# A two-layer graph network with 49 source tiles in place of 50, and one condition an engine at the end

## The reference

```python
# layer 0
h = x @ W + b_W;  xi, xj = split(h, 2)
m = (xj[src] + ea @ W_e + b_We) / (in_degree[dst] + 1e-6)
x1 = layernorm(x + xi + segment_sum(m, dst))
# layer 1: graph convolution with self loops, batch norm over the nodes, leaky ReLU
h = x1 @ W1
dinv = rsqrt(in_degree + 1)
o = segment_sum(h[src] * dinv[src] * dinv[dst], dst) + b1      # self loops included
y = (o - mean) * rsqrt(var + 1e-5) * gamma + beta
out = layernorm(x1 + where(y >= 0, y, 0.01 * y))
```

## Time and profile before

| | |
|---|---|
| median of three runs | 948.84 us (948.3 to 949.46) |
| profiled execution | 947.83 us, span 946.0 us |
| PE busy (matmul) | 895.1 us, 95% of the span, 12296 instructions |
| PE weight loads | 800.0 us, 85% |
| DVE busy | 686.1 us, 73% |
| ACT busy | 465.0 us, 49% |
| POOL busy | 406.1 us, 43% |
| mean granted clock of PE | 0.989 of full speed |
| DMA | 247.94 MB, mean 262 GB/s |

### The profile page before, as it was taken

The page is one execution under the profiler, slowest core; times in us unless marked ns, Lnnn a source line. Parts: engine busy times, 40 slices in busy tenths (PEclk is TensorE's granted clock), DMA queues, the critical chain, the costliest instruction groups (busy, mean ns, idle before and its releaser), DMA issues.

```text
span 946.0 us, 31072 instructions
## 1 busy us (share of the span) xinstructions
PE 895.1 (95%) x12296; PEld 800.0 (85%) x12296; DVE 686.1 (73%) x1587; ACT 465.0 (49%) x991; POOL 406.1 (43%) x495
## 2 busy tenths in 40 slices
PE   5688999999999999999999999999999999999994
PEld 4577888888988988999999999999988988888863
DVE  5898999999999988899888889888822111112254
ACT  3775666666666665566565556566532000000045
POOL 3546755767766654355434445434330110111100
PEclk9899999999999999999999999999999999999997
DMA  5657989888888887777777677779463987788544
GB/s 163 215 210 233 378 296 375 303 311 312 301 287 314 289 310 243 257 246 237 249 265 279 220 256 236 223 266 312 160 262 120 401 321 272 263 294 322 203 146 135
DMA packets 95686, 247.94 MB, mean 262 GB/s; under 512 B 41128, under 2 KB 63356, under 8 KB 89644
## 3 DMA queue, kind: packets, MB, share of 16 engines
q1 hardware_dynamic: 92268, 240.58, 72.4%
q0 software_dynamic: 2400, 4.88, 1.5%
q10 hardware_dynamic: 864, 0.39, 0.2%
HBM read 185.46 MB, written 60.35 MB: 260 GB/s over the span
## 4 chain that ended last, share of the span: by engine, by line
PE 85%; DVE 7%; ACT 3%; DMA 2%; issue 2%; POOL 1%; ACTq 0%; DVEq 0%; POOLq 0%
PE x_ps L809 26%; PE pair_ps L873 19%; PE pair_ps L791 14%; PE e_ps L828 10%; PE x_ps L817 9%; PE j_ps L855 2%; DVE lo_oh L561 2%; DVE key_oh L564 2%; DMA rows<-in_dst,row_i 1%; PE pair_ps L882 1%; PE j_ps L856 1%; ACT counts L993 1%; PE u_vps L1357 1%; DMA xsplit<-in_dst 1%; ACT u_xo L1273 1%
## 5 line engine op out<-in xcount | busy, mean ns | idle before, releaser
L993 ACT CAST counts<-pair_ps 128x800 bf16<-128x800 f32 x391 | 319.5, 830 | 252.0 <-PE pair_ps L791 234.8
L809 PE MATMUL x_ps<-counts,xsplit 128*128 128x256 bf16 (+1 forms) x2500 | 310.9, 270 | 0.0
L561 DVE TENSOR_TENSOR lo_oh<-counter,lo_t 128x1024 bf16<-128x1024 bf16 x391 | 273.3, 699 | 49.9 <-PE pair_ps L791 47.9
L809 PEld LDWEIGHTS x_ps<-counts,xsplit 128*128 128x128 f16 x2500 | 225.7, 97 | 29.8 <-issue 7.9
L564 DVE TENSOR_TENSOR key_oh<-counter,key_t 128x800 bf16<-128x800 bf16 x391 | 233.0, 596 | 0.0
L791 PE MATMUL pair_ps<-key_oh,lo_oh 128*128 128x100 bf16 x3128 | 205.3, 208 | 13.4 <-DVE key_oh L564 6.1
L791 PEld LDWEIGHTS pair_ps<-key_oh,lo_oh 128*128 128x128 bf16 x3128 | 180.2, 97 | 28.6 <-DVE key_oh L564 10.7
L828 PE MATMUL e_ps<-streams 128*32 128x128 f32 x3528 | 108.5, 277 | 0.5 <-issue 0.5
L817 PE MATMUL x_ps<-counts,zown 128*128 128x256 bf16 (+1 forms) x840 | 103.2, 269 | 0.0
L873 PE MATMUL pair_ps<-streams,zown 128*128 128x256 bf16 x904 | 101.8, 273 | 0.0
L828 PEld LDWEIGHTS e_ps<-streams 128*32 128x32 f32 x3528 | 95.0, 111 | 5.4 <-issue 1.5
(11 more groups left out here) (174 smaller groups left out, 881.7 us busy)
## 6 DMA issues: line engine op xcount, KB each, us to landing
streams<-in_edge_attr SPq DMA_DIRECT2D x196, 576.0 KB
counts_kept<-counts SPq DMA_DIRECT2D x10, 1664.0 KB, 8.7
streams<-counts_kept SPq DMA_DIRECT2D x6, 1664.0 KB, 7.0
counts<-counts_kept SPq DMA_DIRECT2D x4, 1664.0 KB, 7.6
counts_kept<-counts SPq DMA_DIRECT2D x2, 3200.0 KB, 13.0
streams<-counts_kept SPq DMA_DIRECT2D x2, 3200.0 KB, 14.6
dinv_row<-dinv_rows SPq DMA_DIRECT2D x25, 128.0 KB, 5.3
edst<-in_dst SPq DMA_DIRECT2D x196, 4.5 KB
```

Source lines behind the costliest of these rows:

```text
L561: dv.tensor_tensor(lo_oh[:, at % RING, :, :, :], counter[:, :, :].unsqueeze(1).to_broadcast([P, SW // 2, P, 2]), pairs(lo_t[b % 2][:, w]). ...
L809: last = nc.tensor.matmul(x_ps[:, 0, 0:n], xsplit[:, q // 2, q % 2, :], by_hi[:, q // 2, :], start=(q == 0), stop=(q == 2 * HI - 1))
L993: a.copy(out.rearrange("p h (g n) -> p h g n", g=2), pair_ps[at % 2][:, :, 0:4 * KW].rearrange("p g (n h) -> p h g n", h=HI)).then_inc(S[" ...
```

## The change

The last block's even and odd nodes go into one tile: even nodes in its partitions 0 to 52, odd ones in 64 to 116. There are HS = 49 tiles, KW = 98 values of the key and 98 passes a block. A key of tile 49 (an odd node of the last block) is drawn to tile 48 with `min`, and 64 is added to its lo. So `make_keys` changes: `dl` is multiplied by HS at once, hi and parity are added first, `upper` marks the odd nodes of the last block, and DVE adds it to lo and writes lo16 itself, at the end; ACT's cast goes. What handled two tiles of the last block handles one (x in three loads, messages into two halves of PSUM, sums, rows, z). `keep_rows` writes that block's rows by two DMAs, one for each half of the tile. For its self loops POOL prepares `itself_last` with a memset and two copies more, ahead of the second layer. At the end the three sections `general`, second finish and last stores are put under one condition for each engine, with general and second finish in it. SP loads the flag after the store of chunk 5, and the stores of chunks 6, 7 and 8 come behind the condition.

```diff
+HS = HI - 1
-KW = 2 * HI
+KW = 2 * HS
-OWN = [(h, min(4, HI - h)) for h in range(0, HI, 4)]
+OWN = [(h, min(4, HS - h)) for h in range(0, HS, 4)]
...
+def tiles(u):
+    return 2 if u < NB - 1 else 1
+def piece_tiles(k):
+    a, z = X_PIECES[k]
+    return slice(2 * a, min(2 * z, HS))
+def x_loads(k):
+    return 1 if k < len(X_PIECES) - 1 else 3
...
-            sp.dma_start(out[0:LAST_P, z - 1 - a, :],
-                         x[(NB - 1) * BN:N, :].rearrange("(p t) f -> p (t f)", t=2)).then_inc(S["x_in"][k], 16)
+            for half in range(2):
+                sp.dma_start(t["x"][64 * half:64 * half + LAST_P, (HS - 1) * F:HS * F],
+                             x[(NB - 1) * BN:N, :].rearrange("(p t) f -> t p f", t=2)[half]).then_inc(S["x_in"][k], 16)
...
             def make_keys(b):
                 dve.wait_ge(win_in[b % 2], 32 * (b // 2 + 1))
                 reach(dve, S["turned"], b)
-                reach(dve, S["lo_float"], b)
+                dv.tensor_scalar(bit_i[:, :], gsrc[b % 2][:, :], 1, None, ALU.bitwise_and)
                 dv.tensor_scalar(hi_i[:, :], gsrc[b % 2][:, :], 7, 62, ALU.logical_shift_right, ALU.bitwise_and)
-                dv.tensor_scalar(dl[:, :], gdst[b % 2][:, :], th[:, b:b + 1], None, ALU.subtract).then_inc(S["dl_made"], 1)
-                dv.tensor_scalar(lo_i[:, :], gsrc[b % 2][:, :], 1, P - 1, ALU.logical_shift_right, ALU.bitwise_and)\
-                  .then_inc(S["lo_int"], 1)
-                dv.tensor_scalar(bit_i[:, :], gsrc[b % 2][:, :], 1, None, ALU.bitwise_and)
+                dv.tensor_scalar(dl[:, :], gdst[b % 2][:, :], th[:, b:b + 1], float(HS), ALU.subtract, ALU.mult)\
+                  .then_inc(S["dl_made"], 1)
+                dv.tensor_scalar(lo_i[:, :], gsrc[b % 2][:, :], 1, P - 1, ALU.logical_shift_right, ALU.bitwise_and)
                 dve.wait_ge(S["dl_made"], b + 1)
-                dv.scalar_tensor_tensor(out=key[:, :], in0=dl[:, :], scalar=float(HI), in1=hi_i[:, :],
-                                        op0=ALU.mult, op1=ALU.add).then_inc(S["key_made"], 1)
+                dv.tensor_tensor(key[:, :], hi_i[:, :], bit_i[:, :], ALU.add).then_inc(S["key_made"], 1)
                 dv.tensor_scalar(junk[:, 0:P], dl[:, :], 0.0, 0.0, ALU.is_equal, ALU.add,
                                  accum_out=deg[:, 2 * b:2 * b + 1])
                 dve.wait_ge(S["key_made"], b + 1)
-                dv.tensor_tensor(key16[:, :], key[:, :], bit_i[:, :], ALU.add).then_inc(S["keyed"], 1)
-                dv.tensor_scalar(junk[:, P:2 * P], dl[:, :], 1.0, 0.0, ALU.is_equal, ALU.add,
-                                 accum_out=deg[:, 2 * b + 1:2 * b + 2]).then_inc(S["deg_known"], 1)
+                dv.scalar_tensor_tensor(out=key16[:, :], in0=key[:, :], scalar=float(HS - 1), in1=dl[:, :],
+                                        op0=ALU.min, op1=ALU.add).then_inc(S["keyed"], 1)
+                dv.tensor_scalar(upper[:, :], key[:, :], float(HS), 64.0, ALU.is_equal, ALU.mult).then_inc(S["lo_int"], 1)
+                last = dv.tensor_scalar(junk[:, P:2 * P], dl[:, :], float(HS), 0.0, ALU.is_equal, ALU.add,
+                                        accum_out=deg[:, 2 * b + 1:2 * b + 2])
+                if b == NB - 1:
+                    step(last)
+                    last = dv.tensor_copy(deg[64:P, 2 * b:2 * b + 1], deg[0:64, 2 * b + 1:2 * b + 2])
+                last.then_inc(S["deg_known"], 1)
+                dve.wait_ge(S["lo_int"], b + 1)
+                dv.tensor_tensor(lo16[:, :], lo_i[:, :], upper[:, :], ALU.add).then_inc(S["lo_float"], 1)
...
-                passes = 2 * HI + early(k)
+                passes = 2 * HS + early(k)
...
-                    nc.tensor.matmul(j_ps[:, t, :], sx[:, t:BN:2], wj, start=True, stop=False)
-                    last = nc.tensor.matmul(j_ps[:, t, :], se[u % 2][:, t:BN:2], we, start=False, stop=True)
+                    out, m = (j_ps[:, t, :], BN) if u < NB - 1 else (j_ps[64 * t:64 * t + 64, 0, :], P)
+                    nc.tensor.matmul(out, sx[:, t:m:2], wj, start=True, stop=False)
+                    last = nc.tensor.matmul(out, se[u % 2][:, t:m:2], we, start=False, stop=True)
...
-            def float_lo(b):
-                act.wait_ge(S["lo_int"], b + 1)
-                reach(act, S["turned"], b)
-                a.copy(lo16[:, :], lo_i[:, :]).then_inc(S["lo_float"], 1)
...
-        LAST_STORES = LC - 1
+            LAST_STORES = LC - 2
...
+        def end_of(engine, name):
+            finish[name](engine)
+            with engine.If(fast[name] < 1):
+                general_parts[name](engine)
+                finish_again[name](engine)
...
+        @block.sync
+        def _(sp):
+            end_of(sp, "sp")
+            last_stores(sp)
```

More of the change, by code:

```diff
@@ L651, in sums @@
                 dve.wait_ge(S["offset_ready"], u + 1)
-                for t in range(2):
+                for t in range(tiles(u)):
                     last = dv.scalar_tensor_tensor(out=v[:, t, :], in0=j_ps[:, t, :], scalar=quot[:, u, t:t + 1],
@@ L1160, with finish_rows @@
                "kept0", "kept1", "kept2", "kept3", "kept_last")
-def finish_rows(nc, block, out, keep, scratch, U, turn, passed, fast):
+def finish_rows(nc, out, keep, scratch, U, fast):
     ident, y, vec, stats, flag = (keep[k] for k in ("ident", "y", "vec", "stats", "flag"))
@@ L1198, in only_if_asked @@
-        def only_if_asked(engine, name):
-            return engine.If(fast[name] < 1) if turn else nullcontext()
-        def load_flag(engine, name):
-            if turn == 0:
-                fast[name] = engine.value_load(flag[0:1, 0:1], min_val=0, max_val=1)
-        def reach_chunk(engine, sem, c):
-            if c > 0:
-                engine.wait_ge(U[sem], c + turn * (LC + 1))
-        @block.sync
-        def _(sp):
-            with only_if_asked(sp, "sp"):
+        v_ps = [ctx.enter_context(nc.psum_tensor(f"u_vps{i}", [P, C, F], F32)) for i in range(VB)]
@@ new lines, in form, with store, load_flag, reach_chunk @@
+        def form(turn, passed):
+            rows = lambda a, z, table: table[a * BN:z * BN, :].rearrange("(b p t) f -> p b (t f)", p=P, t=2)
+            tail = lambda table: table[(NB - 1) * BN:N, :].rearrange("(p t) f -> p (t f)", t=2)
+            size = lambda c: 2 * (CHUNKS[c][1] - CHUNKS[c][0])
+            by_block = lambda buf, c: buf[:, 0:F * size(c)].rearrange("p (b q) -> p b q", q=2 * F)
+            of_buffer = lambda i, n: len(range(i, LC + 1, n))
+            LAST_STORES = LC - 2
+            stored = lambda i: len(range(i, LAST_STORES, XB))
+            x1_of = lambda c: x1_last if c == LC else x1[c % XB]
+            def store(sp, c, done):
+                reach_chunk(sp, "xo_ready", c + 1)
+                if c < LC:
+                    sp.dma_start(rows(*CHUNKS[c], out), by_block(xo[c % XB], c)).then_inc(done, 16)
+                else:
+                    sp.dma_start(tail(out), xo[c % XB][0:LAST_P, 0:2 * F]).then_inc(done, 16)
+            def load_flag(engine, name):
+                if turn == 0:
+                    fast[name] = engine.value_load(flag[0:1, 0:1], min_val=0, max_val=1)
+            def reach_chunk(engine, sem, c):
+                if c > 0:
+                    engine.wait_ge(U[sem], c + turn * (LC + 1))
+            def finish_sp(sp):
@@ L1252, in _, with finish_act @@
                 load_flag(pool, "pool")
-        @block.scalar
-        def _(act):
-            with only_if_asked(act, "act"):
+            def finish_act(act):
                 act.wait_ge(U["batch_root"], 2 * turn + 1)
@@ L1288, in _, with finish_dve @@
                     row_stds(c)
-        @block.vector
-        def _(dve):
-            with only_if_asked(dve, "dve"):
+            def finish_dve(dve):
                 vv = nc.vector
@@ L1334, in _, with finish_pe @@
                         row_scales(c - 2)
-        @block.tensor
-        def _(pe):
-            with only_if_asked(pe, "pe"):
+            def finish_pe(pe):
                 def add_x1(c):
```

489 lines of the change are left out of this document (243 added, 246 removed).

## The result

The changed kernel takes 941.9 us (median of 7 runs, 940.52 to 945.41) against 948.69 us beside it (7 runs, 943.97 to 949.46): ratio 0.9942, 95% interval 0.9921 to 0.9962. Measured again later on another chip it was 0.9943 (0.9920 to 0.9966, 12 runs against 17). By the ratio the gain is 5.5 us (the medians themselves lie 6.8 apart); 11.3 were forecast.

What follows compares the result with a forecast made beforehand. TensorE was taken to bound most of the kernel, with VectorE the tighter of two full engines from 98 to 250 us. The terms -5.3 - 1.1 - 2.0 + 1.0 + 0.4 - 0.3 - 4.0 gave -11.3, so 937.5 us, range 932.5 to 941.5.

Steps and rivals of the forecast that it cites:

- two columns fewer as 0.83 ns a matmul: First layer's counting matmuls: 98 columns instead of 100 save 0.83 ns each, 0.09 us a block over 14 slots.
- Passes removed from slot 15 are free today and bring nothing: First layer: slot 15's passes lie beside ScalarE's chain, so eleven late blocks gain only 0.10 us each, -1.1 us.
- Whole passes a slot: First-layer windows from 250 to 385 us: passes dealt by ceil(passes/15) drop from slots 1 to 14, together -2.0 us.
- +1.0: VectorE's extra make_keys work, net 0.23 us a block, 0.17 of it charged in six uncovered blocks from 98 to 250 us.
- +0.4: Kernel start: lo16 comes later and make_keys(1) is longer, less savings from one tile fewer; +0.4 us.
- Second layer: Each full block loses two passes of source tile 50, all on TensorE's path: -5.3 us.
- The end: SP takes one jump of 2.6 us after chunk 5's store, then three stores, landing at 941.5 instead of 945.6: -4.0 us.
- Rival 3: The end gains little: SP's jump takes 4.0 us and the three stores hold each other up, -1.5; 940.0 us, chance 0.07.
- Everything scales: Rival 1: slot 15's passes do count and VectorE's additions hide, -17.1 us in all; 931.7 us, chance 0.12.
- rivals 2 and 3: Rival 2: VectorE becomes the limit of the first twelve blocks, +0.5 us each; 944.5 us, chance 0.12. Rival 3 has its line.
- Rival 4: Slower than before: key one-hot rows of 98 pairs fall to the fp32 rate on VectorE, +94, some 1043 us; chance 0.04.

Runs made afterwards that it cites:

- e3: Changed kernel with the key one-hot's rows 400 bytes apart in SBUF instead of 392, still 98 columns; one time, 946.1 us beside 950.3 of the kernel before.
- e11: Kernel before (50 tiles, its own end) with passes dealt as 139 over slots 1 to 14 and 9 in slot 15; ratio 0.9981 to the kernel before.
- f2: Changed kernel with key one-hot rows 100 pairs apart and 9 passes dealt to slot 15, both added VectorE instructions kept; 938.37 us, 0.9880 of the kernel before.
- e9: Changed kernel with six more unused VectorE instructions in each block's make_keys, 0.80 us a block; ratio 1.0045 to the kernel before.
- f4: As f2, but without adding the 64 for the upper half, so make_keys has as many VectorE instructions as before; 933.81 us, 0.9829 of the kernel before.
- e7: Changed kernel with one added VectorE instruction replaced by ScalarE's cast and a small matmul that adds the 64; ratio 0.9959 to the kernel before.
- e1: Changed kernel with everything from the finish on (general path, conditions, last stores) as in the kernel before; ratio 0.9965 to the kernel before.
- e4: Changed kernel with 100 columns in the counting matmul and key one-hot rows of 100, 49 tiles of passes kept; ratio 0.9915 to the kernel before.
- e6: Changed kernel with the 146 passes of a block dealt as 137 over slots 1 to 14 and 9 in slot 15; ratio 0.9894 to the kernel before.
- e8: Changed kernel with 100 counting columns, 9 passes in slot 15, and one added VectorE instruction replaced by ScalarE's cast and a small matmul; 934.78 us, 0.9835 of the kernel before.
- e12: As e8, but 98 counting columns with only the key one-hot's rows 100 pairs apart; ratio 0.9888 to the kernel before.
- f3: As f2, but one added VectorE instruction replaced by ScalarE's cast and a small matmul; 935.45 us, 0.9852 of the kernel before.
- e10: Changed kernel with two stores behind its one condition in place of three; one run, 959.6 us with a disturbed block, only its end used.

## Why the prediction was wrong

What failed is the price of the counting matmul in the first layer: taken as 0.83 ns less, it came as 1.5 ns more. The reach of VectorE's added instructions was mis-sized behind it, and smaller terms took the rest: SP's jump and the last landing at the end, one wait in the second layer. The saved passes themselves came as forecast. The two places that were meant to gain big (second layer, end) brought 7.2 of 9.3 us, and the first layer lost 2.6 us where it was to gain 2.0.

**The counting matmuls, "two columns fewer as 0.83 ns a matmul": the sign was wrong, and this is the largest miss.** The forecast drew a line through passes of 112 and 256 columns and read 100 columns off it. The point at 100 happened to lie on it, but 98, 99 and 100 columns all take 45.6 ns: between them the width doesn't count. And the edit that made the matmul narrower also moved the rows it reads from 400 to 392 bytes apart, which costs 1.5 ns in the mean (e3). Per steady block that is +0.15 in place of -0.10 us, and over 16 blocks 4 us; on the table it is the 2.7 us of the third line and the 0.8 of the second. The Trainium skill (TensorE: Matmul & The Clock Gate, Back-to-back issue gap) gives about 81 ns at 128 columns for a stream of weight load and matmul pairs. That figure is far from the 45.6 ns measured here at 98 to 100 columns. What the forecast had inferred from it, that narrower counting matmuls gain nothing, held all the same, and was rejected together with the figure. (It put the difference at 1.2 us; its own terms, 11 x 0.09 and 5 x 0.09, make 1.4.)

**Slot 15.** "Passes removed from slot 15 are free today and bring nothing" held to the last digit: 2.09 us from counts to messages with eight passes and with six, an idle time of 0.31 us at each start of a block (0.2 forecast). What the forecast didn't ask is what that idle time is worth: three passes dealt into it give 0.29 us a block. That is the gain that the change seems to have missed, and e11 shows that most of it needs the change to be had. With the same deal and the same row pitch the 50th tile costs 0.19 us a steady block (27.83 in e11, 27.64 in f2), near the two passes' 0.22. Reading the free slot off equal blocks with 0, 4 and 8 passes was sound.

**Whole passes a slot.** The blocks where ceil(passes/15) fell from ten to nine did shrink: 26.84 to 26.51 and 27.75 to 26.95 us, -1.13 together for -1.28 forecast. The three others were to lose 0.09, 0.31 and 0.31 and changed by +0.10, -0.08 and -0.08: the difference, 0.19 to 0.23 us each, is about the counting term's 0.25 again.

**VectorE, "+1.0" and "+0.4".** The price per block was right (0.33 us of instructions, 0.25 to 0.29 net of the smaller one-hot for 0.23 forecast) and so was the duration of the key one-hot. Its reach was mis-sized: 1.4 us were charged, for six blocks and the start, and e9 and f4 put it at 4.3. The dose shows that the start is the dearest place, and that four blocks behind 250 us pay too. In the traces the start (to the first edge matmul) grew from 48.2 to 50.1 us, and the six blocks behind the third from 151.3 to 152.9: +1.8 and +1.6 for +0.4 and +1.0. The other kernels with both instructions and no dose have it at 49.3 to 51.5 us (eight traces), those with 50 tiles at 48.1 to 49.2 (three), those with one or none of the two at 48.2 to 49.7 (five). e7, with the slower counting matmul and one of the two instructions, has it at 48.2, so the counting is not what delays it. The forecast added up what VectorE gains and loses there, +0.4 in all; of the 1.8 us only 0.3 had come when the first one-hot started (25.62 for 25.28 us). In the profiled execution one stands out: GpSimd's product for the shares took 2.29 us in place of 1.22, another small instruction behind it 2.30 in place of 0.49, and a row lookup was issued 3.5 us later. But e1, e4 and e6 don't show it (1.21 to 1.22) and are as late, so it isn't the cause. How the rest of the start's delay is made up was not settled. Nor do the terms close: 4.3 in place of 1.4 us is 2.9 more, while the profiled pair is 1.8 behind the forecast up to 253 us, and the stretch behind it is accounted for by the counting. The early blocks vary by more than this from trace to trace.

**Second layer.** Each block lost exactly two passes, 0.218 us: 5.2 us. A new wait of 0.85 us gave some back: VectorE's sum for block 24 waits for a transfer issued at 731.57 that needs 10.9 us behind a load of 3.1 MB. In the kernel before the sum was done 0.5 us ahead of its use. Eleven more of the traces with 49 tiles have the wait (0.3 to 0.7 us); e8, e12 and f3 don't, nor do the three with 50 tiles. In e8 and f3, without it, the second layer takes 0.9 us less from its first pass to its last projection than in the changed kernel (184.3 for 185.2). It was not taken away in a run of its own, and why it comes and goes is open.

**The end.** -2.8 for -4.0. Two terms: SP's jump takes 3.0 us in place of 2.6 (branch to first store; 3.0 in every trace of this form but e10, 2.8), and three stores behind it make the last landing 0.7 us longer (e10). Rival 3's shape, at half of its size.

**Chances.** "Everything scales" (0.12) fell, and rivals 2 and 3 each came true by about half, together with a term of which the range knew only the small side. For the counting matmul the bounds were 0 and -3.6; a reason to exclude a loss was not given, and the loss came. Rival 4 asked whether rows of 98 pairs could be dearer, but for VectorE, which writes them, and not for TensorE, which reads them. (Its sum makes +93 us, not +94.)

## What to carry to other kernels

When an edit changes a width, ask what else it moves: the rows' distance in memory is an operand of its own, and padding them back (400 bytes for 392) gave the 0.15 us a block back. Before saving work, find out which slot's work is waited for, and move the saving there: here two passes saved in a covered slot were worth nothing, and three moved into the room they left 0.29 us a block. Price an instruction on a nearly full engine by a dose of it on the chip, since a table of busy shares says where it bounds, but not what a start costs in which three engines wait for each other: there 1.6 us of dose cost 4.8.

## What was not expected of the hardware

- Eight matmuls of 98 columns whose moving rows (the operand that is streamed through, here the key one-hot) lie 392 bytes apart take 0.377 us, at 400 bytes 0.366 (e3); the third and seventh carry most of it, 50 and 49 ns for 45 to 47. 98, 99 and 100 columns make no difference at 400.
- SP's jump over the general path took 2.5 to 2.8 us and the one over the second finish 2.3 (three traces); one jump over both takes 3.0 (2.8 in e10).
- Three stores of 384, 256 and 53 KB in a row land 5.4 to 5.7 us behind the last issue, two of 256 and 53 KB 4.7 to 4.8.
- The program of f3 and e12 is one and the same and was 0.9852 (0.9810 to 0.9894) on one chip and 0.9888 (0.9854 to 0.9922) on another. The intervals overlap, so this need not be the chip; either way, six runs against the kernel before don't tell 0.4%.
